# Attention over eight sequences: batch loops written out, and score products over all 128 rows of the stacks

## What is computed

```python
Q, K, V = (multilora(x, ids, W, A, B) for W, A, B in ((Wq, Aq, Bq), (Wk, Ak, Bk), (Wv, Av, Bv)))
Q, K = rope(split(Q)), rope(split(K))
scores = einsum('bhqd,bhkd->bhqk', Q, K) / sqrt(32)
attn = softmax(where(causal, scores, -inf))
x = layernorm(x + multilora(merge(attn @ split(V)), ids, Wo, Ao, Bo))
```

```python
a = attention(rmsnorm(x, ln1_w), Wq, Wk, Wv, Wo)
mod = 0.1 * tanh(a @ A)
h = rmsnorm(x, ln2_w)
gate = silu(h @ W_in.T + mod * (h @ A) @ B)
x = layernorm(x + x + gate * (h @ W_up.T) @ W_down.T)
```

## Time and profile before

| | us |
|---|---|
| median of three runs | 2967.54 |
| lowest and highest | 2967.21, 2971.47 |
| the profiled execution | 2964.34 |
| its span, first to last instruction | 2962.5 |
| TensorE busy in the span | 2721.6 (92%) |
| VectorE, ScalarE, POOL busy | 1586.3, 1342.3, 645.6 |

### The profile page before, as it was taken

The page is one execution under the profiler, slowest core; times in us unless marked ns, Lnnn a source line. Parts: engine busy times, 40 slices in busy tenths (PEclk is TensorE's granted clock), DMA queues, the critical chain, the costliest instruction groups (busy, mean ns, idle before and its releaser), DMA issues. The chain is left out here.

```text
span 2962.5 us, 46172 instructions
## 1 busy us (share of the span) xinstructions
PE 2721.6 (92%) x13840; PEld 2174.2 (73%) x13840; DVE 1586.3 (54%) x4308; ACT 1342.3 (45%) x2755; POOL 645.6 (22%) x528
## 2 busy tenths in 40 slices
PE   5999999999758999999999994999999999999998
PEld 4778777787636777777777762888888888888886
DVE  3777777777634776777777773422222333333333
ACT  2777677766633666656656664311111231111111
POOL 5455555555321122122122112000000000000000
PEclk8999999999867999999999996999999999999999
DMA  5455555555624544544545543311111121111100
GB/s 140 100 135 132 134 116 133 129 129 116 151 83 118 124 96 115 130 90 112 133 91 118 117 89 97 117 58 49 44 44 44 66 87 46 58 44 45 44 29 29
DMA packets 173888, 276.05 MB, mean 93 GB/s; under 512 B 29204, under 2 KB 53524, under 8 KB 173076
## 3 DMA queue, kind: packets, MB, share of 16 engines
q1 hardware_dynamic: 170772, 260.58, 36.3%
q0 software_dynamic: 2304, 12.58, 1.2%
q10 hardware_dynamic: 640, 1.05, 0.1%
HBM read 97.04 MB, written 42.99 MB: 47 GB/s over the span
## 5 line engine op out<-in xcount | busy, mean ns | idle before, releaser
L2224 DVE TENSOR_TENSOR c_product<-c_up_ps,c_gate 128x512 f32<-128x512 f32 x128 | 88.6, 692 | 653.3 <-PE c_up_ps L2290 653.3
L2278 PE MATMUL c_gate_ps<-c_h_split,c_w_split 128*128 128x512 f32 x1536 | 380.8, 397 | 23.6 <-DVE c_w_split L2176 23.6
L2262 PE MATMUL c_down_ps<-c_w_split,c_product_split 128*128 128x512 f32 x1536 | 379.3, 396 | 0.0
L2290 PE MATMUL c_up_ps<-c_h_split,c_w_split 128*128 128x512 f32 x1536 | 378.2, 395 | 0.0
L2278 PEld LDWEIGHTS c_gate_ps<-c_h_split,c_w_split 128*128 128x128 f32 x1536 | 290.0, 189 | 95.3 <-issue 25.3
L2290 PEld LDWEIGHTS c_up_ps<-c_h_split,c_w_split 128*128 128x128 f32 x1536 | 288.4, 188 | 70.0
L2262 PEld LDWEIGHTS c_down_ps<-c_w_split,c_product_split 128*128 128x128 f32 x1536 | 288.9, 188 | 68.6
L281 ACT ACTIVATE b_prob_hi<-b_scores_t_ps 128x384 fp32r<-128x384 f32 (+1 forms) x384 | 201.1, 524 | 266.0 <-PE b_scores_t_ps L271 230.1
L289 DVE TENSOR_TENSOR b_prob_lo<-b_scores_t_ps,b_prob_hi 128x384 fp32r<-128x384 f32 (+1 forms) x384 | 225.8, 593 | 148.9 <-ACT b_scores_t_ps L282 137.3
L289 DVE TENSOR_TENSOR a_prob_lo<-a_scores_t_ps,a_prob_hi 128x384 fp32r<-128x384 f32 (+1 forms) x384 | 226.2, 593 | 145.3 <-ACT a_scores_t_ps L282 140.3
L2148 ACT ACTIVATE c_gate<-c_gate_ps 128x512 f32<-128x512 f32 x128 | 76.4, 597 | 492.4 <-PE c_gate_ps L2285 492.4
(11 more groups left out here) (205 smaller groups left out, 4969.8 us busy)
## 6 DMA issues: line engine op xcount, KB each, us to landing
a_q_stack<-a_q_split SPq DMA_DIRECT2D x192, 128.0 KB, 3.2
a_k_stack<-a_k_split SPq DMA_DIRECT2D x192, 128.0 KB, 3.5
b_q_stack<-b_q_split SPq DMA_DIRECT2D x192, 128.0 KB, 3.3
b_k_stack<-b_k_split SPq DMA_DIRECT2D x192, 128.0 KB, 3.6
c_h_stage<-h_t SPq DMA_DIRECT2D x16, 1024.0 KB, 6.2
c_res<-x SPq DMA_DIRECT2D x16, 1024.0 KB, 5.5
c_w_stage<-in_mlp_w POOLq DMA_DIRECT2D x16, 768.0 KB, 4.5
stage<-in_x_t SPq DMA_DIRECT2D x8, 1024.0 KB, 6.4
```

Source lines behind the costliest of these rows:

```text
L2224: dve.tensor_tensor(product[:, bank, :], up_ps[:, bank, :], gate[:, bank, :], ALU.mult).then_inc(product_done, 1)
L2262: mm = pe.matmul(down_ps[:, t, :], product_split[:, kt % 2, a, t * P:t * P + P], w_split[:, w, kt, 2 * KC * P:], start=(kt == 0 and i == 0 ...
L2278: pe.matmul(gate_ps[:, bank, :], w_split[:, w, ft, c * 2 * P:c * 2 * P + P], h_split[run.pair][:, a, c, :], start=(c == 0 and w == 0 and a ...
L2290: mm = pe.matmul(up_ps[:, bank, :], w_split[:, w, ft, c * 2 * P + P:(c + 1) * 2 * P], h_split[run.pair][:, a, c, :], start=(c == 0 and w = ...
```

## The change

It does four things. `batches` writes out all eight batches, for all five engines in both attention stages, so that no engine jumps and all awaited values become constants. Both score products read all 128 rows of the stacks. So that the max pass adds nothing from the shift rows, `stack_send` has a seventh transfer for each pair, between those of the queries and those of the keys: it copies two rows that are always zero (116 and 117) over rows 112 and 113 for the pair's two heads, four pieces of 2048 bytes, 8 KB. All waits on `stacked` count 112 for each group instead of 96. And because the copied rows must have been cleared, SP's wait for POOL's `rows_zeroed` at the start of either stage asks for two more of the four clearings.

```diff
-SPLIT_ROWS, SHIFT_ROW, STACK_ROWS = 112, 112, 114
+STACKED = 7 * 16
+SHIFT_ROW, SHIFT_END, SPARE_ROW = 112, 114, 116
...
 def batches(eng, body, ahead=1):
-    body(0)
-    with eng.Fori(1, BATCH - ahead) as b:
-        body(b)
-    for b in range(BATCH - ahead, BATCH):
+    for b in range(BATCH):
         body(b)
...
-        pe.wait_ge(at.stacked[h // 2], n * 96 + 96)
+        pe.wait_ge(at.stacked[h // 2], n * STACKED + STACKED)
...
-        mm = pe.matmul(at.scores_ps[:, k % 2, col:col + width], q[0:SPLIT_ROWS, h, qt * P:qt * P + P],
-                       key[0:SPLIT_ROWS, h, 0:(qt + 1) * P], start=(i == 0), stop=True, skip_group_check=True)
+        mm = pe.matmul(at.scores_ps[:, k % 2, col:col + width], q[:, h, qt * P:qt * P + P],
+                       key[:, h, 0:(qt + 1) * P], start=(i == 0), stop=True, skip_group_check=True)
...
                      at.q_split[rows, part, :].bitcast(F32)).then_inc(at.stacked[pair], 16)
+    sp.dma_start(q[SHIFT_ROW:SHIFT_END, heads, :].bitcast(F32),
+                 q[SPARE_ROW:SPARE_ROW + SHIFT_END - SHIFT_ROW, heads, :].bitcast(F32)).then_inc(at.stacked[pair], 16)
     apart(sp, at.ones_set, at.k_ready, n + 1)
...
-        pe.matmul(at.scores_t_ps[:, k % 2, col:col + width], key[0:STACK_ROWS, h, kt * P:kt * P + P],
-                  q[0:STACK_ROWS, h, kt * P:SEQ], start=(i == 0), stop=False, skip_group_check=True)
+        pe.matmul(at.scores_t_ps[:, k % 2, col:col + width], key[:, h, kt * P:kt * P + P],
+                  q[:, h, kt * P:SEQ], start=(i == 0), stop=False, skip_group_check=True)
...
-            sp.wait_ge(rows_zeroed, 2)
+            sp.wait_ge(rows_zeroed, 4)
...
-            sp.wait_ge(rows_zeroed, zeroed_before + 2)
+            sp.wait_ge(rows_zeroed, zeroed_before + 4)
```

More of the change, by code:

```diff
@@ L744, in rotated_hi @@
                 for pair in range(2):
-                    at_least(act, at.stacked[pair], n * 96)
+                    at_least(act, at.stacked[pair], n * STACKED)
                 split = at.k_split if i else at.q_split
```

2 lines of the change are left out of this document (1 added, 1 removed).

## The result

The changed kernel takes 2940.08 us (median of four runs, 2937.65 to 2947.83) beside 2967.38 for the kernel before on the same chip: a ratio of 0.991, 95% interval 0.9889 to 0.9931. It is 27 us faster. The profiled execution took 2941.34 us, with a span of 2939.4 us, where the kernel before had 2964.34 and 2962.5.

The account below looks back on a forecast made before the run. TensorE's work was taken to set the time, leaving its idle time and slower clock to gain; terms summing to -17.4 took the profiled 2964.3 us to 2946.9, 2950 on the median's scale, range 2936 to 2963.

Parts of the forecast that it names:

- The gate stage's loops: Gate stage, step g = 0 after four jumps: without VectorE's late instruction 113.7 us fall to 4 x 24.2, -16.9 us.
- The attention stage's loops: Attention stage, step g = 0 after five jumps: 129.8 us fall to 127.0, a gain of 2.8 us.
- whole difference: Rival: attention stage gives all 12.7 us, since a jump puts SP and POOL out of step; 2940 us, chance 0.18.
- Register instructions: Looped batches, both stages: VectorE's 27 waits before a maximum go, mostly hidden behind TensorE's work; gain 1 us.
- 128 rows: Score products of both stages: reading 128 rows takes as long as 114, so 0, between -6 and +4 us.
- The clearings: Seventh transfer of each `stack_send`: holds SP some 0.6 us, so keys leave later; +3.3 us in all.
- The wait for POOL: Start of both stages: SP waits for all query clearings, which end before SP comes there; cost 0.
- The slower rival, SP's queue as the bound: Slot 1: TensorE waits for pair 0's keys in every step, 62 x 0.6 = 37 us; 2984 us, chance 0.07.
- The threshold: Loss in the average step, 0.4 us, from which the slower SP queue would decide the result.
- Late instructions in straight code: Rival: written-out batches meet the same 2.7 us stall elsewhere; 2971 us, chance 0.12 shared with small terms eating the gain.
- More than 15 us of waits for stacks: Sign of being wrong: in the profile after, the waits for the stacks grow beyond 15 us in all.
- New waits on issue in straight code: Sign of being wrong: waits put down to "issue" turn up in the written-out code of the profile after.

Follow-up runs that it names:

- vector_only: The kernel before with the batch loops written out for VectorE alone; 2958.4 us, ratio 0.9981.
- all_but_vector: The kernel before with the batch loops written out for the four engines other than VectorE; 2953.2 us, ratio 0.9965.
- unroll_only: The kernel before with only the batch loops written out, for all engines; 2940.9 us, in a repeat 2937.3 us.
- narrow_clear: The changed kernel with both score products back at 112 and 114 rows, seventh transfer kept; 2945.8 us, ratio 0.9936.
- clear4: The changed kernel with three more small zero transfers in each send, ten for each pair; 3091.6 us, ratio 1.0426.
- wide_t: The changed kernel without the seventh transfer, transposed scores over 128 rows, max pass over 112; 2931.3 us, in a repeat 2933.3 us.
- wide_gate: As wide_t, but with 128 rows in the transposed scores of the gate stage only, 114 in the attention stage; 2935.3 us.
- mlp_too: wide_t with the MLP stage's loops written out as well; 2932.4 us, ratio 0.9902.

## Why the prediction was right, step by step

- **The gate stage's loops, -16.9.** Right in size. Over the six steps g = 0 the trace lost 16.9, and six written-out kernels without clearings have a gate stage of 839.9 us in the mean, 16.8 less than 856.7. The two of them with nothing but the loops written out have 838.8 and 847.6, so the stage by itself gives the term to within some 5 us. But the working named one cause where there were two: it put the stall down to VectorE and looked at ScalarE only as what might come up later. vector_only and all_but_vector show that either engine's stall alone costs the whole. The sum was right because the change takes away both, which is luck in so far as the working had not looked for the second.
- **The attention stage's loops, -2.8.** Too small. The six kernels have 762.9 us in the mean, 8.3 less than 771.2; 4.9 of that is in the steps g = 0 (155.2 to 150.3), where I had 2.8, since batch 1, which I took as the measure of "no jump", gets faster too (25.4, then 24.6 in unroll_only). The other 3.4 are in the steps that I didn't count, for fear of counting the clock. The fear was not idle: the six had 46.2 us at the slower clock in that stage in the mean, and the kernel before 51.2. The 8.3 lie about midway between my 2.8 and the 12.7 of the rival "whole difference", and the time fell into that rival's case (2935 to 2943), which had a chance of 0.18. Its mechanism, SP and POOL out of step for the whole batch, no run shows.
- **Register instructions, -1.** Not separable: they are part of these 8.3 us. The 18.4 us of VectorE's waits are gone, and nothing of that size came out at TensorE, as the working had it.
- **128 rows, 0.** Right for the length of the products (414 and 225 ns, were 414 and 227). But the kernels with 128 rows in both stages ran 4 to 10 us faster than their like with a higher granted clock, which a term of 0 doesn't have; the cause is open. In the change this about cancels the clearings: the loops alone took 2940.9 and 2937.3, the change 2940.1 and 2938.3.
- **The clearings, +3.3.** The size is near (5.5 by the stages' means, 4.9 by narrow_clear), the place is not. SP's 0.6 us were 0.68 (266.18 to 266.86). But I asked only who waits for the stacks. TensorE's waits for keys rose by 1.2 us, about the 1.4 forecast, but in 11 waits, where I had one in a batch. The cost lies at `gather`, two issues further down the same queue, which I named nowhere; ScalarE waits for it with the exponentials behind. In the gate stage it is 0.4, where I had 1.3. ScalarE's wait did grow from 5.6 to 9.8, but it is 8.0 to 9.1 in the six kernels without clearings as well, so the clearings added about 1.4 us to it and the written-out loops the rest. TensorE's part is the 0.4.
- **The wait for POOL, 0.** Nothing in the profile speaks against it: the stretch ahead of the first transposed score took 73.8 us, was 73.1, and the one between the stages 100.8, was 101.9.
- **The slower rival, SP's queue as the bound.** It didn't happen with one added transfer and did with four. The threshold was set at 0.4 us for a step; the change lost 5.5 / 62 = 0.09, clear4 153 / 62 = 2.5 more.
- **Late instructions in straight code.** They did not come: no wait of VectorE on "issue" in either attention stage, and ScalarE's seven are the old 1.5 us under another name.
- **The marks.** "More than 15 us of waits for stacks" was to prove me wrong. They are 9.1 + 1.6 on TensorE and 9.8 on ScalarE, 20.5 us, and the kernel is faster all the same, so that mark was badly chosen: before they had been 7.9 + 1.3 + 5.6 = 14.8 already. "New waits on issue in straight code" was met by its wording too, by ScalarE's seven, and meant nothing. The clock fell in one step where it had not in the kernel before (attention stage, batch 0, g = 1, 3.4 us) and in fewer steps in all.

Put together for the profiled execution: -16.8 and -8.3 for the loops, +5.5 for the clearings, -19.6 in all, where the spans differ by 23.1. The rest is in the stages that the change leaves alone (2.0 us) and in the gate stage's clock: its steps g = 2 had 34 us at the slower clock in six batches before and 14 after. The steps g = 2 of batches 1 and 2, before and then after:

```profile
1108.00:1136.60 28.60, 26.38 (x136) 20.62 (x137) 20.64 (x58) 19.98 (x42) 7.09 (x5) 0.88 0.52 123
1221.40:1248.70 27.30, 25.37 (x136) 19.52 (x137) 20.28 (x58) 19.94 (x42) 7.66 (x5) 0.94 0.54 128
```

```profile
1106.20:1134.30 28.10, 25.38 (x137) 19.59 (x138) 21.46 (x58) 20.00 (x42) 7.18 (x5) 0.94 0.50 126
1214.70:1241.60 26.90, 24.23 (x136) 18.17 (x137) 21.47 (x58) 19.73 (x42) 7.20 (x5) 1.00 0.53 132
```

TensorE meets the same waits at the start of the steps at 1108.0 and at 1214.7 (1.36 and 0.4 us), and the clock falls in the one and not in the other. The runs don't show why.

The prediction missed the median by 10 us (2950 against 2940.1). Of these, 2.2 are the terms: 4.5 too little for the loops and register instructions of the attention stage (3.8 against 8.3), 2.2 too little for the clearings, which works the other way, and 0.1 too much for the gate stage's loops (the sum was -17.4, and the measured terms give -19.6). 3.5 are the clock and the stages left alone (19.6 to 23.1). The terms measured here are means over kernels of which most have 128 rows in one stage or both, so what the rows bring is in them and can't be told apart. And 4.3 lie between the profiled executions and the medians: the kernel before has its median 3.0 above its profiled execution, which I carried over, and the changed one 1.3 below.

## What to carry over

When two engines of a chain are late at the same jump, taking away the lateness of one gains nothing, as vector_only and all_but_vector show in the gate stage; look at each engine's first instruction after its branch, and write out the loops of all that are late. For every transfer put into a queue, go down the queue until it next has idle time, and ask of each item there who waits for it, also who waits to overwrite what it reads. A first small transfer can be nearly free while the next ones cost ten times as much, so measure with a multiple before adding more. And before a difference between kernels is put down to the spread of the clock, compare the granted clock of all their executions, not of the profiled one alone.

## What the runs showed of the hardware

- After a jump back in the attention stages VectorE's next instruction came 3.0 to 4.0 us after the branch, at all nine jumps; ScalarE's 3.1 to 3.4 us at four and 0.2 us at five. TensorE (0.06 us), POOL (0.1) and SP (0.2 to 0.3) went on. In the MLP stage, with a loop body of 99 and 94 instructions, VectorE's and ScalarE's came after 0.1 to 0.3 us.
- Two engines late at the same jump cost TensorE what one costs: the gate stage's six steps g = 0 took 161.5 us with both late, 160.3 and 161.4 with one, 145 with none.
- A transfer of 8 KB within the on-chip memory held the issuing queue for 0.64 us, as long as one of 128 KB (1.83 for three).
- Instructions of the same stage, run in the same order, had between 27.3 and 37.5 us at TensorE's slower clock in three profiled kernels (wide_t, its repeat, wide_gate), which moved the stage by up to 3 us.
- The mean granted clock of a whole execution went from 0.960 to 0.970 among 29 executions of kernels with all loops written out and no clearings (unroll_only, wide_t, their repeats and mlp_too), and was higher in those with 128 rows (0.966 in the mean) than in those with 114 (0.963).
